# The second norm of a scan and mixture-of-experts kernel, run by parts of 512 tokens in every batch

## The reference, cut to what matters

```
mod = (silu(c) @ wmod)  ->  sa, ca, ga, sb, cb, gb      # ga, gb: sign kept, magnitude at least 0.25
h = layernorm(x) * (1 + ca) + sa                         # the first norm
x_dbl = h @ W_x.T ; dt = softplus(x_dbl[:64] @ W_dt.T + b_dt)
state[t] = exp(dt * A) * state[t-1] + dt * h * B[t]      # 16 states for each feature
x = x + ga * (sum_n state * C + h * D)
h = layernorm(x) * (1 + cb) + sb                         # the second norm
p = softmax(h @ Wg) over 8 experts; the best 2 get gates that sum to 1
x = x + gb * sum_e gate_e * (h @ We[e] + be[e])
```

## Time and profile before

| | |
|---|---|
| runs | 1143.65, 1139.85, 1138.73 us; median 1139.85 |
| profiled execution | 1137.84 us, of which span 1135.8 us |
| busy | DVE 990.9, POOL 934.9, PE 917.4, ACT 781.4 us |
| mean granted TensorE clock | 0.875 |
| first DVE multiply to the last scan's end | 31.1 to 1027.5 us |
| last scan's end to the end of the span | 108 us |

### The profile page before, as it was taken

The page is one execution under the profiler, slowest core; times in us unless marked ns, Lnnn a source line. Parts: engine busy times, 40 slices in busy tenths (PEclk is TensorE's granted clock), DMA queues, the critical chain, the costliest instruction groups (busy, mean ns, idle before and its releaser), DMA issues. The chain is left out here.

```text
span 1135.8 us, 14810 instructions
## 1 busy us (share of the span) xinstructions
PE 917.4 (81%) x4187; PEld 581.1 (51%) x4203; DVE 990.9 (87%) x1294; ACT 781.4 (69%) x1618; POOL 934.9 (82%) x373
## 2 busy tenths in 40 slices
PE   6336544699788988899879988899879988699998
PEld 4002111266555655456545656465536655366886
DVE  2799999999999999999999999999999999994200
ACT  5686789588967898588866897688867595442100
POOL 2376667699989999699988999799979998897553
PEclk9556665599999998899899998999889999899999
DMA  4925241627155534546174635556271716411222
GB/s 124 237 62 140 59 111 38 168 84 194 54 136 159 148 103 102 160 108 171 47 169 125 162 83 130 135 138 151 57 188 48 195 47 150 120 34 62 69 85 71
DMA packets 89793, 131.28 MB, mean 116 GB/s; under 512 B 13280, under 2 KB 73256, under 8 KB 89200
## 3 DMA queue, kind: packets, MB, share of 16 engines
q1 hardware_dynamic: 89712, 130.34, 44.8%
HBM read 54.50 MB, written 8.65 MB: 56 GB/s over the span
## 5 line engine op out<-in xcount | busy, mean ns | idle before, releaser
L1104 POOL TENSOR_TENSOR h<-h,Cr 128x2048 f32<-128x2048 f32 (+1 forms) x131 | 582.0, 4444 | 36.4 <-DVE h L989 13.1
L676 PE MATMUL ps<-xg,we 128*128 128x256 f32 x2048 | 492.5, 397 | 6.4 <-POOL xg L1138 3.6
L676 PEld LDWEIGHTS ps<-xg,we 128*128 128x128 f32 x2048 | 399.8, 199 | 88.6 <-issue 28.4
L724 ACT ACTIVATE av<-dd,An 128x512 f32<-128x512 f32 x512 | 351.0, 714 | 70.6 <-DVE h L989 64.4
L1138 POOL TENSOR_TENSOR xg<-h2T,gbc 128x1024 f32<-128x1024 f32 x128 | 303.3, 2372 | 59.0 <-PE ps L676 42.2
L976 DVE TENSOR_TENSOR ps<-ps,dd 128x512 f32<-128x512 f32 x512 | 326.4, 684 | 3.3 <-DMA dd<-src 2.8
L989 DVE TENSOR_TENSOR_SCAN h<-av,kept,ps 128x512 f32<-128x512 f32 x256 | 313.5, 1264 | 3.1 <-PE ps L569 2.5
L989 DVE TENSOR_TENSOR_SCAN h<-av,ps 128x512 f32<-128x512 f32 x256 | 298.0, 1204 | 11.1 <-PE ps L569 8.3
L569 PE MATMUL ps<-h,gam 128*32 128x512 f32 x1024 | 157.1, 741 | 53.6 <-POOL h L1104 25.2
L569 PEld LDWEIGHTS ps<-h,gam 128*32 128x32 f32 x1024 | 31.1, 124 | 134.4 <-issue 99.9
L1011 DVE TENSOR_TENSOR X<-ps,X 128x512 f32<-128x512 f32 x32 | 21.7, 679 | 64.1 <-PE ps L647 64.1
(11 more groups left out here) (105 smaller groups left out, 812.1 us busy)
## 6 DMA issues: line engine op xcount, KB each, us to landing
dd<-src SPq DMA_DIRECT2D x480, 128.0 KB, 2.4
gbc<-gates SPq DMA_DIRECT2D x128, 256.0 KB, 3.4
X<-in_x SPq DMA_DIRECT2D x8, 1024.0 KB, 6.9
out<-X SPq DMA_DIRECT2D x32, 256.0 KB, 3.5
XN<-in_x SPq DMA_DIRECT2D x7, 1024.0 KB, 7.3
dd<-src SPq DMA_DIRECT2D x16, 256.0 KB, 5.0
we<-in_We SPq DMA_DIRECT2D x2, 1024.0 KB, 10.8
XN<-in_x SPq DMA_DIRECT2D x2, 512.0 KB, 4.5
```

What stands on the lines that cost most here:

```text
L676: e = pe.matmul(bk[:, m * 256:(m + 1) * 256], we[:, hf, 2 * ep + e2, m * P:(m + 1) * P], xg[:, i % XG, e2, hf], start=(ep == e2 == m == hf ...
L724: act.activation(av[:, u % AS], step_of(u, 0), ACT.Exp, scale=An[:, 0, i:i + 1]).then_inc(s_a, 1)
L1104: pool.tensor_tensor(hu, hu, Cr[:, q:q + 1].to_broadcast([P, n, CH]), ALU.mult).then_inc(s_ch, n)
```

## The change

The norm of the last batch was already done by parts of 512 tokens. Now every batch does it so. `rstd 1` becomes two steps a batch, each over four columns, and so does `rsb 1`; the eight small operations of `rsb 1` stay eight. Three due times are new, `earlyX`, `earlyR` and `earlyT` (with variants P, A and B): they bring normalisation, `rstd`/`rsb` and transposes of part 0 forward against those of part 1. The waits count parts in place of batches (`normed`). And nearly every number of the table `AT` is another one, so steps change place on every engine, the start included. Of the table two lines stand below.

```diff
-AT = dict(exp=-0.93, mul=0.17, scan=0.35, ch=7.15, Bs=-2.04, y=7.82, stat0=-4.25, stat0s=0.64, rstd0=9.17,
+AT = dict(earlyX=4.69, earlyR=7.65, earlyT=2.63, earlyXP=6.86, earlyRP=5.94, earlyTP=1.94, earlyXA=-5.51,
...
-        put(t + times["xh1"] + i * times["xh1s"] + i // 4 * times["xh1g"], "xh", 1, b, k)
-    put(t + times["rstd1"], "rstd", 1, *tag)
-    put(t + times["rstd1"] + times["rsb1"], "rsb", 1, *tag)
+        put(t + times["xh1"] + i * times["xh1s"] + i // 4 * times["xh1g"] - (0 if i > 3 or b == LAST else times["earlyX"]),
+            "xh", 1, b, k)
     for i, c in enumerate(halves):
+        s = t + times["rstd1"] - (0 if i or b == LAST else times["earlyR"])
+        put(s, "rstd", 1, b, c)
+        put(s + times["rsb1"], "rsb", 1, b, c)
         for hf in range(2):
-            s = t + times["xT1"] + times["xT1s"] * i + times["xT1h"] * hf
+            s = t + times["xT1"] + times["xT1s"] * i + times["xT1h"] * hf - (0 if i or b == LAST else times["earlyT"])
...
         def normed(w, b, c=0):
 
             if w:
-                return LAST + c + 1 if b == LAST else b + 1
+                return 2 * b + c + 1
             return b + 2 if b else c + 1
...
-                    if k == 0 or k == 4 and by_dve(w, b):
+                    if k % 4 == 0 and (w or k == 0 or by_dve(w, b)):
                         act.wait_ge(s_rs[w], normed(w, b, k // 4))
...
-                        act.wait_ge(s_sq[w], 8 * (b + 1 if w else b))
-                        act.activation(ln, rs[:, w, 1], ACT.Ln, bias=eps[:], scale=1.0 / D).then_inc(s_ln[w], 1)
+                        act.wait_ge(s_sq[w], 8 * b + k1 if w else 8 * b)
+                        act.activation(ln, rs[:, w, 1, k0:k1], ACT.Ln, bias=eps[:], scale=1.0 / D).then_inc(s_ln[w], 1)
```

More of the change, by code:

```diff
@@ new lines @@
+AT = dict(earlyX=4.69, earlyR=7.65, earlyT=2.63, earlyXP=6.86, earlyRP=5.94, earlyTP=1.94, earlyXA=-5.51,
+          earlyXB=8.89, earlyRA=6.38, earlyRB=-3.08, earlyTA=5.99, earlyTB=-21.21, exp=-0.98, mul=0.25, scan=0.33,
+          ch=6.93, Bs=-1.15, y=7.71, stat0=-3.99, stat0s=0.53, rstd0=7.1, rsb0=2.5, xh0=9.71, xh0s=0.36, xT0=16.18,
+          xT0h=1.6, xTs=3.09, rxT0=0.21, wx=3.65, rwx=0.59, S=-0.46, ldx=33.54, gam=41.81, dl0=21.73, dl1=32.66,
+          dls=1.82, rdl=1.22, sp=1.77, dt=10.64, C=24.8, CS=3.73, rC=0.94, ddt=36.57, ddts=0.49, ddu=37.55, ddus=0.78,
+          zs=4.71, ldx2=28.21, z=4.63, zX=0.33, stat1=4.96, stat1s=0.34, rstd1=9.65, rsb1=1.1, xh1=10.97, xh1s=0.31,
+          xh1g=-1.03, xT1=10.19, xT1h=0.21, xT1s=2.69, rxT1=0.9, lg=13.78, rlg=1.02, lT=0.01, soft=0.61, softe=0.79,
+          top=0.8, gT=1.23, rgT=1.07, gw=8.92, gr=23.68, xg=22.82, xgs=1.77, gl=-0.35, f=-2.93, fE=1.3, o=0.98,
+          oX=1.42, out=12.04, md1=0.22, gates=0.3, ga=-2.93, stat1A=8.0, stat1B=6.76, stat1sA=21.65, stat1sB=13.8,
+          rstd1A=11.35, rstd1B=6.01, rsb1A=0.15, rsb1B=5.32, xh1A=12.26, xh1B=12.46, xh1sA=0.88, xh1sB=0.38,
+          xh1gA=-1.32, xh1gB=30.58, xT1A=15.04, xT1B=12.87, xT1hA=0.54, xT1hB=0.01, xT1sA=35.14, xT1sB=-7.43,
+          rxT1A=0.45, rxT1B=2.28, lgA=20.32, lgB=14.58, rlgA=0.96, rlgB=4.88, lTA=0.32, lTB=4.77, softA=1.22,
+          softB=0.3, softeA=-0.02, softeB=21.86, topA=1.25, topB=4.05, gTA=5.57, gTB=6.35, rgTA=5.2, rgTB=16.35,
+          gwA=23.69, gwB=20.91, grA=47.16, grB=38.56, xgA=37.88, xgB=34.0, xgsA=1.27, xgsB=1.85, glA=-7.75, glB=-5.12,
+          fA=-3.6, fB=-4.4, fEA=21.95, fEB=41.29, oA=2.7, oB=4.09, oXA=30.87, oXB=28.04, outA=24.86, outB=24.42,
+          stat1P=5.66, stat1sP=0.18, rstd1P=7.91, rsb1P=1.19, xh1P=11.55, xh1sP=0.06, xh1gP=2.01, xT1P=10.23,
+          xT1hP=-0.0, xT1sP=3.09, rxT1P=0.66, lgP=13.96, rlgP=0.81, lTP=0.11, softP=0.63, softeP=0.24, topP=1.19,
+          gTP=0.95, rgTP=0.14, gwP=11.64, grP=34.34, xgP=22.74, xgsP=1.78, glP=-3.31, fP=-2.42, fEP=0.44, oP=1.35,
+          oXP=0.37, outP=19.59, rstd0H=-6.27, xh0H=3.8, xh0sH=1.52, xT0H=1.87, xT0hH=2.69, xTsH=13.26, rxT0H=0.82,
+          wxH=8.87, rwxH=2.92, SH=0.45, dlsH=0.03, rdlH=3.27, dtH=11.18, CH=26.85, CSH=0.85, rCH=0.97, dl0H=21.7,
+          ldxH=22.2, dduH=21.7, ddusH=0.12, stat0F=6.18, stat0sF=0.51, rstd0F=10.34, rsb0F=0.04, xh0F=13.51,
+          xh0sF=0.1, rS=30.94, rSH=-11.41, seed=7.39, x=16.32, mean=13.22, prime=-20.38, early=5.95, earlyP=9.03,
+          earlyA=39.15, earlyB=-49.01, halfH=8.42, bn0H=-0.15, rsb0H=2.37, sel=-36.97, mdr=-24.51, BsH=-8.74,
+          we=-3.01, openY=1.17, openX=14.81)
```

## The result

| | before | changed |
|---|---|---|
| median (runs) | 1139.29 us (1138.70 to 1143.65, 4 runs) | 1154.65 us (1153.64 to 1155.62, 4 runs) |
| profiled execution | 1137.84 us, span 1135.8 | 1153.64 us, span 1151.9 |
| scan 16 starts | 66.97 | 72.69 (+5.7) |
| last scan ends | 1027.54 | 1037.46 (+9.9, so 4.2 in the body) |
| from there to the end of the span | 108.3 | 114.4 (+6.1) |

The ratio is 1.0126, interval 1.0099 to 1.0154: slower by more than I forecast, and outside my range (1137.5 to 1152). The start came as written, the body and the end didn't. The profiled execution of the kernel before, 1137.84 us, is at the fast end of its kernel: 44 later executions beside the experiments took 1137.76 to 1144.24, so distances between its trace and another can overstate a loss by some 3 us.

A forecast was written before the change was run, and what follows sets the result against it. DVE was taken as the bound, working almost without pause from first multiply to last scan. 1137.84 + 6.2 (start) + 0 (body) + 0 (end) = 1144.0; the median lies 2.0 above, so 1146.0 us, range 1137.5 to 1152.

The forecast's parts named there:

- Step 1: Start: ACT's two read-outs of part 1 ahead of softplus's table load make `dt 0 0` and the DMAs behind it 1.45 us later.
- Step 2: Start: late `md 1` and the gates put scan 0 near 38 instead of 34.74, costing 0 beyond the first step.
- Step 3: Start: `gam 0` ahead of `ch 7` on POOL delays y 0; scan 16 comes 6.2 us later, the 1.45 included.
- The norm by parts itself: 0: Seven more `rstd`, 4 us on ACT, are hidden by ACT's idle time and cost 0.
- Body 0: Scans after the start: +1.8 us from y 33 and -1.8 from `fE` ahead of `gT`'s read-out; bounds -15 and +8.
- y 32 late: Body: seeds some 1.6 us later nearly use up y 32's slack of 1.9; 0 to 0.5 lost per batch, taken as 0.
- y 33 later: Body: `oX 2 2` 1.2 later, transposes give back 1.0; net 0.2 to 0.3 later, six times, +1.8 us.
- The body wins: Rival, chance 0.20: transposes between f and y 32 keep PE at 2.4 GHz, holds of four batches go; 1137.5, at best 1131.
- The body loses: Rival, chance 0.15: y 32 late by 0.5 and slow `f` in all six batches; +8.1, with the start +14.3, 1154.
- The end 0, within 1.5: After the last scan: last `fE` about -0.6, batch 7's transposes and `o 6 3` each up to +1; taken as 0.

The follow-up runs named there:

- parts_old_order: Changed code with the table of the kernel before and the three new due times at zero, so all steps in the old order; 1146.39 us, ratio 1.0056.
- parts_rstd_late: parts_old_order with the second `rstd` moved behind the two seeds in batches 1 to 5; 1146.53 us, ratio 1.0054.
- after_stats_late: Changed kernel with part 0's four `stat 1` behind the read-out of `dl` on ACT in batches 1 to 5; 1156.22 us, ratio 1.0157.
- before_o2_late: Kernel before, with transposes `o b-2 2` behind `f b-2 3 0` and `oX b-2 2` three scans later, batches 2 to 7; 1138.02 us, ratio 0.998.
- before_filled_o: Kernel before, plus 8, 4, 12 or 6 identity transposes on PE ahead of its wait at each `o`, up to batch 5; 1150.06 us, ratio 1.0072.
- the joined repairs: Changed kernel with `ch 7` ahead of `gam 0`, `stat 1` behind the read-out of `dl`, and `o b-2 2` behind `f b-2 3 0`; 1151.33 us, ratio 1.0082.

## Why the prediction was wrong

**Start, right.** Step 1: `dt 0 0` at 23.15 (23.04 written). Step 2: scan 0 at 38.66 (38), unit 6 still waits for its DMA, the late `md 1` costs 0. Step 3: `gam 0` at 63.50 (64.0), y 0 at 68.98 (69.5), scan 16 at 72.69 (73.2). +5.7 for 6.2; the experiments put 4 to 5 of it on `gam 0`. The multiply of unit 6 came at 48.79 for 48.0, and the way from `gam 0` to scan 16 took 9.19 for 9.2. That POOL's queue would not hold scan 24 was right too.

**"The norm by parts itself: 0", wrong.** This is the first failed step. ACT's idle time was to hide seven `rstd`; the bare edit in the old order costs 5 to 6 us (parts_old_order, parts_rstd_late). The price isn't the operations' own 4 us in line: batches that took 126 take 126.3, and the two of 123.4 became 126.3 and 126.5. I had read the body from its waits in total and never cut it by batch, so I did not see that the kernel before had two lengths of batch, nor that ACT's average idle time says nothing of what a shift of half a microsecond does there. What is lost is the batches in which the clock recovers halfway through `f b-2 3 0`. In the kernel before the fall begins 31.0, 30.4, 30.7, 30.8 and 30.3 us into batches 2 to 6, so its place moves from batch to batch, and now and then a batch is short; in parts_rstd_late it begins 31.1, 30.9 and then three times 30.8 us in and lasts through most of the product each time, and in parts_old_order the falls stand elsewhere but repeat in every batch to 0.1 us. Why these repeat and never give a short batch stays open, and so does what the split costs in the changed order: no run has the changed table without it.

**"Body 0", wrong by 4 us, and by its steps.** y 32 late: no. y 33 later: no, its holds fell from 6.8 us in four to 2.2 in four. The read-out of `C` and `dl` behind the four `stat 1`: I had not followed these, and they are the 10 us of `zX`. Yet this wasn't the price either, since after_stats_late took 7 of them away for nothing. The sums of the waits moved; the length of the batch, about 126, did not. (The four `xh 1` less one `rstd` are 4 x 0.49 - 0.5 = 1.46, where I wrote 1.6; nothing hangs on it.)

**The rivals.** "The body wins" named the right place and the wrong effect: the holds at y 33 shrank here and went in before_o2_late and before_filled_o, and only before_o2_late gained anything, in some executions. "The body loses" came nearest in size (1154), in part by luck: y 32 was not late, and its end of 0 isn't what was measured. Its slow `f` in every batch is what parts_rstd_late shows; in the changed kernel the same `f` takes 5.3 to 5.4 us in three batches and full speed in two, with other products slow in their place.

**"The end 0, within 1.5", wrong: +6.1.** I gave the transposes ahead of y 62 up to 1; they and their read-outs behind them cost 2.6. The other 3.4 is the lower clock at two products, which the order alone doesn't set: the kernel before has it too in some traces of its own order.

**Sum.** start 5.7 + body 4.2 + end 6.1 = 16.0 of the span, against 6.2 + 0 + 0: the forecast of 1144.0 for a profiled execution fell 9.6 short of 1153.64, nearly all of it body and end. By experiments: `gam 0` about 5, the norm by parts in itself 5.6, the end's order 2.7; these 13 leave 2 to 3 for the rest, which no single run isolates. The terms aren't independent, as the joined repairs show, and the 5.6, a difference of medians, may hold part of the end's 3.4.

## What to carry to other kernels

Cut a repeating stream by its period before pricing an edit: if equal iterations have two lengths, an edit of nearly nothing can cost the difference in every short one, and the totals of waits won't show it. A wait that goes is a gain only if no other engine is a microsecond behind it: count the period, not the wait. Look at several traces of one order before a difference of 3 us between two orders is put down to the order. And ask, of two instructions that change places, behind which of them another engine's DMA or sum is hidden, as `ch 7` behind the gates' DMAs.
